# A Mamba scan beside a mixture of experts: the loop written out, the first scan unit put first, lists loaded by blocks

## What is computed

```python
xn = _layernorm(x)
# scan branch: rows sorted by cluster, then for every position of the sorted sequence
dA = jnp.exp(d_t[..., None] * A)                      # (B, 256, 16 states)
h = dA * h + (d_t * u_t)[..., None] * b_t[:, None, :]
y = jnp.einsum('bdn,bn->bd', h, c_t)
y = y + D[None, :, None] * u                          # the D times row term, then unsorted
# expert branch: two of 8 experts for each token
h = silu(xt @ w1[e]) * (xt @ w3[e])
y = h @ w2[e]                                         # weighted by probs, added up
out = x + scan + experts
```

## Time and profile before

| | us |
|---|---|
| median of 3 runs (range) | 818.84 (816.11 to 818.92) |
| profiled execution, its own time | 817.38 |
| its span, first to last instruction | 815.3 |
| VectorE busy | 682.9 (84%) |
| TensorE busy | 663.9 (81%) |
| GpSimd busy | 597.3 (73%) |
| ScalarE busy | 431.0 (53%) |
| preparation, until | about 155 |
| scan stage, first scan to last reduce | 172.1 to 747.1 |
| tail | 747.1 to 815.3 |

### The profile page before, as it was taken

How to read it: one execution, slowest core, us unless ns; L and a number is a source line. 1 busy time by engine, 2 the same in 40 slices (tenths; PEclk the granted TensorE clock), 3 DMA queues, 4 the chain that set the end, 5 groups by cost and what they waited for, 6 DMA issues and landing times. The chain is left out here.

```text
span 815.3 us, 15751 instructions
## 1 busy us (share of the span) xinstructions
PE 663.9 (81%) x4538; PEld 422.7 (52%) x4539; DVE 682.9 (84%) x882; ACT 431.0 (53%) x926; POOL 597.3 (73%) x372
## 2 busy tenths in 40 slices
PE   3734889788998798989998898999889798989870
PEld 2523745245655465556655565565556555655550
DVE  5769777579999999999999999999999999997110
ACT  1324656465655556656655575566557554653320
POOL 3728800038788898988989898888989898889532
PEclk9866955599999989999999998999999998999995
DMA  7972659979944754674575466547645654662322
GB/s 228 371 259 91 180 206 297 321 221 241 210 102 103 144 118 87 146 150 94 115 163 111 89 149 138 105 90 164 139 90 125 134 127 90 142 142 35 49 27 26
DMA packets 76845, 118.63 MB, mean 146 GB/s; under 512 B 22456, under 2 KB 56848, under 8 KB 74512
## 3 DMA queue, kind: packets, MB, share of 16 engines
q1 hardware_dynamic: 54656, 90.95, 41.2%
q0 software_dynamic: 19824, 27.16, 19.4%
q10 hardware_dynamic: 2336, 0.15, 0.2%
HBM read 82.87 MB, written 35.27 MB: 145 GB/s over the span
## 5 line engine op out<-in xcount | busy, mean ns | idle before, releaser
L534 POOL TENSOR_TENSOR ring<-ring,bc 128x1024 f32<-128x1024 f32 (+2 forms) x128 | 308.0, 2424 | 38.9 <-DVE state L1047 38.0
L1044 DVE TENSOR_TENSOR_SCAN ring<-ring,state,pb 128x512 f32<-128x512 f32 x256 | 313.8, 1267 | 4.6
L654 ACT ACTIVATE ring<-late,aneg 128x512 f32<-128x512 f32 x256 | 164.2, 721 | 12.0 <-DMA late<-dd_d 9.1
L1035 DVE TENSOR_TENSOR pb<-fb,bc 128x1024 f32<-128x1024 f32 x128 | 157.3, 1229 | 3.0
L1284 PE MATMUL py<-w2x,pool 128*128 x568 | 141.6, 395 | 0.5 <-ACT pool L726 0.3
L1267 PE MATMUL fa<-w,pool 128*128 x284 | 137.7, 608 | 3.9 <-issue 2.8
L506 POOL DMA_INDIRECT out_dram<-pool,meta x71 | 112.9, 1590 | 29.8 <-issue 15.7
L1267 PE MATMUL fb<-w,pool 128*128 x284 | 134.3, 596 | 0.0
L486 POOL DMA_INDIRECT pool<-xn_d,meta x71 | 71.3, 1004 | 81.3 <-DVE ids L1001 33.5
L1284 PEld LDWEIGHTS py<-w2x,pool 128*128 128x128 f32 x568 | 107.7, 200 | 13.6 <-issue 1.0
L1267 PEld LDWEIGHTS fb<-w,pool 128*128 128x128 f32 x284 | 54.5, 192 | 68.9 <-issue 68.9
(11 more groups left out here) (213 smaller groups left out, 752.8 us busy)
## 6 DMA issues: line engine op xcount, KB each, us to landing
late<-dd_d SPq DMA_DIRECT2D x256, 128.0 KB
bc<-bc_d SPq DMA_DIRECT2D x72, 256.0 KB
w<-in_L_ffn_w_dram SPq DMA_DIRECT2D x16, 512.0 KB, 8.6
ring<-in_L_attn_x_dram SPq DMA_DIRECT2D x8, 512.0 KB, 4.3
out_dram<-ring SPq DMA_DIRECT2D x8, 512.0 KB, 7.7
xn_d<-w2x SPq DMA_DIRECT2D x8, 512.0 KB, 8.6
dd_d<-pool SPq DMA_DIRECT2D x8, 512.0 KB
dd_d<-ring SPq DMA_DIRECT2D x8, 512.0 KB, 5.1
```

The costliest lines, as they stand in the source:

```text
L534: ins = po.tensor_tensor(r, r, c_rows, ALU.mult)
L654: ins = ac.activation(ring[:, g % RING, n, :], dd[:, g % 2, 0, :], ACT.Exp, scale=aneg[:, NH * g + n:NH * g + n + 1])
L1035: ve.tensor_tensor(pb[:, :].rearrange("p (n c) -> p n c", n=2), pd[:, :].rearrange("p (o c) -> p o c", o=1).to_broadcast([P, 2, CH]), b_ro ...
L1044: ve.tensor_tensor_scan(r, r, pb[:, CH * m:CH * m + CH], state[:, NH * g + n:NH * g + n + 1], ALU.mult, ALU.add).then_inc(S["scan_done"], 1)
```

## The change

1. The loop is written out: every engine has the 64 units as plain code. The experts lag two units further: VectorE makes the silu row of expert u - 1 before unit u, and unit 0 comes ahead of every silu row. Eight experts' silu rows follow the last unit, where there were six.
2. ScalarE's copy and exponentials of unit 0, and the exponentials of unit 1, come before the first tanh, and each waits for less: unit 0 for VectorE's last product of the preparation, unit 1 for one of the stores that read ring slot 1, unit 2 for the other.
3. `meta` holds 16 experts in two blocks of 8. A block is one load. Blocks 0 and 1 are loaded in the preparation, block c + 1 by SP at step 7 of turn c. Gathers run six experts ahead in six buffers (before: four).
4. `ya` has two buffers and `hand_over` is gone. Three `ye` buffers instead of two.
5. From expert 63 on TensorE no longer adds the D times row term; VectorE multiplies the gathered row by weight and D (`skip_row`) and puts it to the result while it takes that out of PSUM (`take_out`). From expert 65 on the silu rows are turned between the `fa` and `fb` products. VectorE makes half of the last unit's multiply by C.
6. The last four scan adds go without waiting for one another, after expert 65. SP no longer waits for TensorE's turns, and loads weights of one expert per step, without a wait of its own.

The places of the order that matter:

The core of the diff:

```diff
-                    load_meta(j + 3, (s + 4) % SPI, s % 2)
-                    if 3 <= s < 3 + P // DG:
-                        load_bc((c + 1) % NCH, (c + 1) % 2, [s - 3])
+            for u in range(UNITS):
+                c, g = u // G, u % G
+                if u >= 2:
+                    load_dd(u)
+                if c == 0 and g + EARLY < E:
+                    load_up(g + EARLY, w3, w3_in)
+                    load_down(g + EARLY)
+                if g == 4 and c + 1 < NCH:
+                    if c:
+                        sp.wait_ge(S["hc_done"], G * c)
+                    sp.wait_ge(S["bc_in"], 128 * (c + 1))
+                if g >= 4 and c + 1 < NCH:
+                    load_bc(c + 1, g - 4)
+                if g == 7 and c:
+                    sp.wait_ge(S["meta_in"], 16 * (c + 1))
+                    sp.wait_ge(S["added"], landed_expert(BLOCK * c - 1))
+                    load_meta(c + 1)
...
+            def gather(j):
+                po.wait_ge(S["meta_in"], 16 * (j // BLOCK + 1))
+                if j >= XR:
+                    po.wait_ge(S["xtr_done"], j - XR + 1)
...
+            for u in range(UNITS):
+                c, g = u // G, u % G
+                j = u - 2
+                if j >= 0:
+                    gather(j + XR)
+                scans = SCAN_UNITS.get(g, ()) if c else ()
+                split = 1 if scans else NH // 2
+                po.wait_ge(S["h_ready"], u + 1)
+                done = multiply(u, slice(0, split))
+                for n in scans:
+                    add_scan(c - 1, n, landed_scan(c - 1, scans[0]) - 16)
...
+                if j >= 0:
+                    add_expert(j)
+            for j in range(UNITS - 2, FT):
+                if j + XR < FT:
+                    gather(j + XR)
+                add_expert(j)
+                if j == LAST_SCANS:
+                    for n in range(TPC):
+                        add_scan(NCH - 1, n, landed_expert(j))
...
+            def exps(u):
+                ac.wait_ge(dd_in[u % 2], 64 * (u // 2 + 1))
+                if u == 0:
+                    ac.wait_ge(S["pr_du"], KC * NCH)
+                elif u == 1:
+                    ac.wait_ge(S["bc_put1"], 32 * NCH // 2)
+                    ac.wait_ge(S["dd_put10"], 16 * NCH // 2)
+                elif u == 2:
+                    ac.wait_ge(S["dd_put11"], 16 * NCH // 2)
...
+            for u in range(UNITS):
+                if u:
+                    silu(u - 1)
+                half_unit(u, 0)
+                half_unit(u, 1)
+                keep_states(u)
...
+            for j in range(TAIL, FT):
+                skip_row(j)
+                silu(j)
+                if j > TAIL:
+                    take_out(j - 1)
+            take_out(FT - 1)
```

More of the change, by code:

```diff
@@ L491, in _ @@
             po.wait_ge(S["pr_ids"], NCH - 1)
-            gather(0, 0)
-            gather(1, 1)
+            gather(0)
+            gather(1)
             for h in range(KC):
                 po.wait_ge(S[f"dd_put0{h}"], 16 * NCH // 2)
-            gather(2, 2)
-            gather(3, 3)
-            def add_expert(turn, j, slot, parity):
-                po.wait_ge(S["ye_done"], j + 2)
-                if not isinstance(j, int):
-                    apart(po)
-                po.wait_ge(S["added"], landed(turn - 1))
-                apart(po)
-                po.indirect_dma_start(out[:, :], bass.IndirectOffsetOnAxis(ap=meta.bitcast(U32)[:, slot, 0:1], axis=0),
-                                      ye[:, parity, :], None, compute_op=ALU.add).then_inc(S["added"], 16)
@@ L509, in add_scan @@
-            def add_scan(turn, c, n, beside=0):
-                po.wait_ge(S["yb_done"], c + 1)
-                if not isinstance(c, int):
-                    apart(po)
-                po.wait_ge(S["added"], landed(turn - 1 - beside))
-                apart(po)
-                po.indirect_dma_start(out[:, :], bass.IndirectOffsetOnAxis(ap=idb[:, n:n + 1], axis=0), yb[:, n, :], None,
-                                      compute_op=ALU.add).then_inc(S["added"], 16)
-            po.wait_ge(S["acc_put"], 16 * NCH)
@@ L521, in turn @@
-            def turn(c):
-                for s in range(SPI):
-                    gather(SPI * c + 4 + s, (s + 4) % SPI)
-                    po.wait_ge(S["h_ready"], unit_index(c, s) + 1)
-                    if not isinstance(c, int):
-                        apart(po)
-                    adds = [n for n in range(TPC) if SCAN_STEPS[n] == s and not isinstance(c, int)]
-                    split = 1 if adds else NH // 2
-                    for states in (slice(0, split), slice(split, NH)):
-                        c_rows = bc[:, 0, 1, states, :].rearrange("p n c -> p (n c)") if isinstance(c, int) else \
-                            bc[:, bass.ds(c % 2, 1), 1, states, :].rearrange("p o n c -> p (o n c)")
-                        r = ring[:, s % RING, states, :].rearrange("p n c -> p (n c)")
-                        ins = po.tensor_tensor(r, r, c_rows, ALU.mult)
-                        if states.start == 0:
-                            for k, n in enumerate(adds):
-                                add_scan(expert_turn(c, s) - len(adds) + k, c - 1, n, k)
-                    ins.then_inc(S["hc_done"], 1)
-                    add_expert(expert_turn(c, s), SPI * c + s, s, s % 2)
@@ L541, in _ @@
-            turn(0)
-            with po.Fori(1, NCH) as c:
-                turn(c)
-            for i, (kind, n) in enumerate(REST_ADDS):
-                if kind == "expert":
-                    if n + 4 < FT:
-                        gather(n + 4, (n + 4) % SPI)
-                    add_expert(REST_TURN + i, n, n % SPI, n % 2)
-                else:
-                    add_scan(REST_TURN + i, NCH - 1, n)
-            po.wait_ge(S["added"], landed(REST_TURN + len(REST_ADDS) - 1))
+            for j in range(2, XR):
+                gather(j)
@@ L724, in evac_ht, with evac_y @@
             def evac_ht(j):
                 ac.wait_ge(S["htr_done"], j + 1)
+                if j == 0:
+                    ac.wait_ge(S["bc_put0"], 32 * NCH // 2)
                 ac.copy(ht, pt[:, :]).then_inc(S["ht_done"], 1)
[L728 removed]
+            def evac_y(j):
                 ac.wait_ge(S["w2_done"], j + 1)
[L730 to L732 removed]
@@ new lines, in evac_y @@
+                ac.activation(ye[j % YE], py[:, 0:D], ACT.Copy, scale=meta[:, j % (2 * BLOCK), 1:2]).then_inc(S["ye_done"], 1)
+            ac.sem_inc(S["ye_done"], 1)
+            put_du(0)
+            exps(0)
+            evac_xt(0)
+            exps(1)
+            for u in range(1, FT + 1):
+                j = u - 1
+                tanh(j)
+                if u < UNITS:
+                    put_du(u)
+                if j:
+                    evac_ht(j - 1)
+                if 3 <= u < UNITS + 3:
+                    take_y(u - 3)
+                if 2 <= u < UNITS + 2:
+                    take_sum(u - 2)
+                if j + 1 < FT:
+                    evac_xt(j + 1)
+                if u + 1 < UNITS:
+                    exps(u + 1)
+                if j and j <= TAIL:
+                    evac_y(j - 1)
```

513 lines of the change are left out of this document (210 added, 303 removed).

## The result

The changed kernel takes 825.45 us (median of 4 runs), the kernel before beside it 818.28: 1.0093 times (95% interval 1.0068 to 1.0118): slower by 0.9%, where 809.5 and faster was forecast. Its profiled run took 824.44 with a span of 822.7.

A forecast was written before the change was run, and what follows sets the result against it. VectorE's pace bounds the scan stage, with the start before it and the chain of adds into `out` after it. -6.8 - 8.0 + 5 + 0.5 = -9.3 us: profiled 817.38 becomes 808.1, median 809.5, range 802.5 to 818.

The forecast's parts named there:

- Part 1, the start: Start of the kernel, up to unit 2's reduce: forecast at 189.3 against 196.14, -6.8 us (-8.0 to -5.1).
- Part 2, the pace: Scan stage on VectorE: written-out units take 8.89 us each, where they took 9.03; -8.0 us.
- the longer code might not stream: Rival: TensorE's listing grows from 744 to 1804 rows, each unit loses 0.35, +22 us, 832; chance 0.05.
- Part 3, the wait: GpSimd waits at step 4 of turns 1 to 7 for the expert list; some 0.9 in six turns, +5 us.
- the 1.4 until packets move: In the list's landing time: some 1.4 us estimated from SP's first issue until its packets move.
- The limit is R + 10.4: TensorE's fold may start 10.4 us after its unit's reduce before VectorE stalls; stall of 0.8 at unit 4.
- it ends at 6.5 - 3.3 + 8.4 = R7 + 11.6: GpSimd's unit 7, with two scan adds, takes 8.4 us and ends 11.6 after that unit's reduce.
- Part 4, the tail: After unit 63's reduce the chain of adds ends the kernel: last add at +60.2 against +59.7, +0.5 us.
- take-over of the D row: Tail: dropping TensorE's D product is worth nothing, since the chain of adds covers it.
- the earlier turn: Tail: turning the silu rows earlier on TensorE is worth nothing, since the chain of adds covers it.
- The rivals: Four alternatives: list in time 0.22, no change 0.14, slower by the list 0.07, longer code not streaming 0.05.
- the rival to which I gave 0.07: Slower by the list: it lands 8 us after unit 4's reduce, stalls 21.6 us, time 826; chance 0.07.

## Why the prediction was wrong

**Part 1, the start: right.** R2 was forecast at 189.3 and is 189.65. ScalarE's table load stands behind the second exponentials (167.06), and the exponentials of unit 2 wait 8.01 for `dd` at 177.75, forecast 177.0. The steps before it were less exact, and did not matter: the first `du` copy is at 159.27 and not 157, and R1 at 177.82 and not 179.3.

**Part 2, the pace: right.** 8.89 or 8.90 in every interval without a stall, from R2 to R13 without one. That the longer code might not stream has nothing to show for it.

**Part 3, the wait: right in place and time, wrong in price.** The gather starts at R4 + 5.4 to 6.7 in the six turns (forecast + 5.5), in turn 7 at + 2.6 (+ 3.1). The list put two transfers earlier is issued 0.9 earlier and lets the gather go 2.8 earlier in turn 1. The rule of the Trainium skill that SyncE's ring on each DMA engine is consumed in order (DMA: Bandwidth & Descriptors, Queues, rings and completion order) fits this, but no run tells it from the mere sharing of full DMA engines. No row shows the 1.4 until packets move, an estimate in the sum; what shows is an issue at R4 + 0.9 to 1.3 and a landing at + 5.1 to 6.5. The multiply ends at R4 + 11.2 (forecast 11.2), GpSimd regains 1.1 a unit as forecast (R13 + 10.05), and the fold of step 7 starts at R7 + 9.2 to 11.8 (forecast 11.6). But the stalls come to 20.7 us, not 5.

The step that failed is "The limit is R + 10.4": it took the way from the fold to the `fb` product as a constant 6.2, from one row at full clock. The number itself holds: F + d - 16.6 is nothing at F = 10.4 when d is 6.2. But d is 6.2 at full clock only, and at d = 9.0 the limit is 7.6. In the nine stalls d was 6.18 to 9.63. Read for every turn, and not once, the fold of step 3 in the trace of before, always at F = 8.76 with waits of 1.1 to 3.3, has d = 8.49, 7.78, 7.61, 9.16, 6.22, 6.20 and 5.74: the row that I took is the sixth turn's, one of the three in which the clock held, and the first and the fourth cost 0.6 and 1.3 us of stall even there.

A second step failed beside it: "it ends at 6.5 - 3.3 + 8.4 = R7 + 11.6, over the limit by a little more than the unit 4 stall had already given back". The 3.3 is right (GpSimd's 23.3 us against three units of 8.89), but the unit took 9.3 and 9.5 and not 8.4 from multiply to fold in turns 1 and 2, since its first scan add waited 1.09 and 1.18, where 0.15 was the wait before. So step 7 pays by itself (1.17, 4.25 and 2.85 in three turns).

The stalls of 20.7 us are then: 5 as forecast; 8 to 10 by my estimate above, since the lateness costs a second time behind the scan adds of step 7, and since the multiply ended at 12.4 and 11.9 and not 11.2 in two turns, and turn 4 began late at step 3 (F = 10.94; GpSimd's gather there starts 2.0 later than in turn 3); and 6 to 7 by the clock. With each F as measured the last two are 5 and 11. What the runs show is the sum, the rule and the d of each row; how much the clock alone added stays open between the two. The Trainium skill (TensorE: Matmul & The Clock Gate, HAM oscillation — how this bites in real kernels) has a kernel whose matmuls wait for a transfer at every block and so start every block at half rate; this trace agrees, with 0.50 behind the wait for GpSimd at 391.86.

**Part 4, the tail: right.** The last add is at R63 + 60.26, forecast + 60.2:

```profile
804.09 0.48 DVE L1038 SCALAR_TENSOR_TENSOR pool<-py,meta,pool 128x256 f32<-128x256 f32 x1 [3.81 <-DMA out_dram<-pool,meta]
...
813.44 1.55 POOL L470 DMA_INDIRECT out_dram<-pool,meta  x1 [2.89 <-DMA out_dram<-pool,meta]
```

VectorE's take-over of the D row ends in a wait for an add, and adds end the tail. So it is worth nothing here, as the earlier turn is; for the take-over that is read from this trace, not tested.

**The rivals.** The time is that of the rival to which I gave 0.07, but not by its condition: it had the list at R4 + 8. It came at + 5.5, where I had it.

## What to carry to other kernels

A wait on a path with slack can cost more than its lateness less the slack, where the waiting engine is TensorE: measure the time behind the wait in the turns in which it already waits, not in a busy one. A list that is loaded in blocks must be issued by the time of its first reader, and the reader may run several steps ahead; here the same change with the list issued ahead of that step's `bc`, or of its `dd` too, is 0.992 and 0.987 of the kernel before, and beats both. A stall saved early in a turn is no gain while the late engine stays late: follow it to the next place where it is waited for. An edit that shortens a late engine's path once but makes its round longer than the pace keeps it late.

## What the runs showed of the hardware

In the changed kernel the granted clock fell to 0.50 for a few us behind all six folds that had kept TensorE idle for 2 us and more (0.50 in 394 to 399), with the same products at 3.62 and not 1.89 us. The length of the one wait does not decide it: with the list held back it stayed at full speed behind five waits of 2.09 to 2.94, and it fell behind a wait of 0.66 in the changed kernel (turn 2, step 3, d 8.17) and of 0.44 in the kernel before (turn 6, step 7, d 9.06). So one row says little. Where products whose results nobody reads left 0.8 to 1.2 us idle, it held. The same kernel's time differs by chip: the kernel before took 809.5 to 820.2 us on them, and two of its traces 4.5 us apart by R0.
